# Where a Fourier layer's sixteen pixel transposes stand: twelve ahead of the forward stage, four inside it

## The reference, cut to what matters

```python
x = coords @ fc0_w + fc0_b                       # (32, 64, 64, 3) -> 32 channels
for sw, cw, cb in the four layers:
    x_ft = rfft2(x);  out = einsum('bixy,ioxy->boxy', x_ft[:, :, :20, :20], sw)
    x = gelu(irfft2(out) + einsum('bchw,oc->bohw', x, cw) + cb)      # exact gelu
x = gelu(x @ fc1_w + fc1_b) @ fc2_w + fc2_b      # one value per pixel
h = concat(cls_tok, x);  h += attention(layernorm(h));  h += experts(layernorm(h))
```

## Time and profile before

| | |
|---|---|
| median of 3 runs | 1129.65 us (1129.07 to 1131.33) |
| the profiled execution's own time | 1131.64 us |
| its span, first to last instruction | 1129.8 us, so 1.84 us lie around it |
| PE, DVE, ACT, POOL busy | 1024.6, 614.7, 410.1, 137.2 us |
| mean granted TensorE clock | 0.978 |

### The profile page before, as it was taken

The page is one execution under the profiler, slowest core; times in us unless marked ns, Lnnn a source line. Parts: engine busy times, 40 slices in busy tenths (PEclk is TensorE's granted clock), DMA queues, the critical chain, the costliest instruction groups (busy, mean ns, idle before and its releaser), DMA issues.

```text
span 1129.8 us, 36328 instructions
## 1 busy us (share of the span) xinstructions
PE 1024.6 (91%) x16860; PEld 654.0 (58%) x16860; DVE 614.7 (54%) x773; ACT 410.1 (36%) x554; POOL 137.2 (12%) x127
## 2 busy tenths in 40 slices
PE   4899899899989999999899899889999899689996
PEld 3676567567657633676576667567325788632221
DVE  2258455825844221458248455923144577769887
ACT  2332233223223486232232233223585778421100
POOL 6000000000000000000000000020000665334421
PEclk9999999999999999999999999999999899879998
DMA  5220130022021300310220130020011000000000
GB/s 187 89 75 3 62 94 12 3 89 75 3 74 53 115 6 22 118 32 3 89 75 3 44 103 21 3 90 16 2 25 43 1 1 2 2 1 1 1 10 10
DMA packets 25660, 46.75 MB, mean 41 GB/s; under 512 B 9437, under 2 KB 10488, under 8 KB 24869
## 3 DMA queue, kind: packets, MB, share of 16 engines
q1 hardware_dynamic: 24694, 43.49, 12.6%
q10 hardware_dynamic: 384, 0.66, 0.2%
q0 software_dynamic: 432, 0.29, 0.1%
HBM read 30.25 MB, written 10.89 MB: 36 GB/s over the span
## 4 chain that ended last, share of the span: by engine, by line
PE 69%; DVE 14%; issue 6%; ACT 4%; DMA 3%; POOL 2%; SPq 1%; ACTq 0%; POOLq 0%; DVEq 0%
PE PSALL L1288 22%; PE PSALL L1256 7%; DVE WORK L1494 6%; PE PSALL L1366 4%; PE PSALL L1279 4%; PE PSALL L1232 4%; PE PSALL L517 4%; PE PSALL L1151 3%; PE PSALL L1376 3%; PE PSALL L1165 3%; PE PSALL L420 3%; DMA WORK<-MIXED 2%; PE PSALL L505 2%; DVE WORK L1513 2%; PE PSALL L399 2%
## 5 line engine op out<-in xcount | busy, mean ns | idle before, releaser
L1513 DVE STREAM_TRANSPOSE WORK<-PSALL 128x1024 f32<-128x1024 f32 x128 | 152.4, 1230 | 292.9 <-PE PSALL L1256 292.9
L1288 PEld LDWEIGHTS PSALL<-EW,WORK 64*128 64x128 f32 x4096 | 250.0, 193 | 65.5 <-issue 48.3
L1288 PE MATMUL PSALL<-EW,WORK 64*128 64x128 f32 x4096 | 266.1, 283 | 12.8 <-DVE WORK L1513 12.8
L1416 ACT ACTIVATE X<-PSALL,TABLES 128x1024 f32<-128x1024 f32 x128 | 141.7, 1114 | 331.6 <-PE PSALL L1288 331.6
L1494 DVE STREAM_TRANSPOSE WORK<-PSALL 128x1024 f32<-128x1024 f32 x84 | 102.3, 1223 | 26.8 <-PE PSALL L1151 26.8
L1397 ACT COPY SPEC<-PSALL 128x400 f32<-128x400 f32 x64 | 53.9, 851 | 152.7 <-PE PSALL L1165 149.8
L1165 PEld LDWEIGHTS PSALL<-TABLES,WORK 128*64 128x64 f32 x2000 | 67.0, 138 | 65.7 <-DVE WORK L1494 53.2
L1165 PE MATMUL PSALL<-TABLES,WORK 128*64 128x64 f32 x2000 | 80.7, 228 | 23.1 <-DVE WORK L1494 19.9
L1485 DVE STREAM_TRANSPOSE WORK<-X 128x1024 f32<-128x1024 f32 x78 | 92.8, 1207 | 16.4 <-PE PSALL L1288 16.4
L1151 PE MATMUL PSALL<-WORK,DW 32*64 32x256 f32 x2496 | 95.8, 391 | 0.0
L697 POOL MEMSET SW<- 64x4160 f32 x1 | 3.6, 3559 | 725.0 <-PE PSALL L1240 725.0
(11 more groups left out here) (156 smaller groups left out, 1059.1 us busy)
## 6 DMA issues: line engine op xcount, KB each, us to landing
SW<-in_spec_w SPq DMA_DIRECT2D x160, 80.0 KB, 2.7
spec_scr<-MIXED SPq DMA_DIRECT2D x24, 400.0 KB, 3.3
SPEC<-spec_scr SPq DMA_DIRECT2D x32, 200.0 KB
WORK<-spec_scr SPq DMA_DIRECT2D x16, 200.0 KB
WORK<-MIXED SPq DMA_DIRECT2D x64, 40.0 KB
WORK<-in_coords_w SPq DMA_DIRECT2D x2, 1024.0 KB, 4.8
XC<-in_coords_c SPq DMA_DIRECT2D x2, 1024.0 KB, 7.2
hid_scr<-WORK SPq DMA_DIRECT2D x64, 8.0 KB
```

Of the source, the lines that this page charges most:

```text
L1288: m = pe.matmul(PS[2 * p + z][:, 2 * b * GRID:(2 * b + 2) * GRID], G[64 * z:64 * z + 64, n % 2, b, h:h + 4, :, c].rearrange("p q o -> p (q ...
L1416: nc.scalar.activation(X[:, n].rearrange("p b (z d) c w -> p d z b (c w)", z=2)[:, p, :, :, 2 * t * GRID:2 * (t + 1) * GRID], PSALL[:, 2 * ...
L1513: nc.vector.transpose(G[:, n % 2, 2 * x + y].rearrange("p h o v -> p o h v"), PSALL[:, 4 + 2 * x:6 + 2 * x, :].rearrange("p k (h o v) -> p ...
```

## The change

Twelve pixel transposes stand in the inverse stage: images 2 and 3 in slots 3 and 4, images 0 and 1 in slot 5, 4 and 5 in slot 6, and 6 to 11 in the last slot. The other four follow the row transposes of images 1, 4, 7 and 10. Each image of the first fourteen has a home of its own: a new tile `XPS` of 3 x 1024 columns is added for images 2 to 4 (and again 14, 15), images 0 and 1 lie in `work[:, 8192:10240]`, 5 to 7 in `MIXED`, 8 to 13 in `work[:, 0:6144]`. The waits follow the homes. As the order of the transposes is no longer that of the images, PE's waits go by `pixels_done`. The scratch for dynamic DMA is set to 4096 instead of being left at its default.

```diff
-EARLY, XP_RING = 3, 6
-PIXELS_IN_INVERSE = [[], [], [], [], [0, 1], [2], [], [3, 4, 5, 6]]
-PIXELS_AFTER = [[], [7], [8], [9], [10], [11], [12], [13], [14], [15], [], [], [], [], [], []]
+SPARE = 3
+PIXELS_IN_INVERSE = [[], [], [], [2], [3], [0, 1], [4, 5], [6, 7, 8, 9, 10, 11]]
+PIXELS_AFTER = [[], [12], [], [], [13], [], [], [14], [], [], [15], [], [], [], [], []]
+PIXEL_ORDER = [k for slot in PIXELS_IN_INVERSE + PIXELS_AFTER for k in slot]
...
+def pixels_done(k):
+
+    return max(PIXEL_ORDER.index(i) for i in range(k + 1)) + 1
...
-        pixel_homes = ([MIXED[:, 1024 * i:1024 * i + 1024] for i in range(EARLY)]
-                       + [work[:, 1024 * i:1024 * i + 1024] for i in range(XP_RING)])
-        XP = [(pixel_homes[k] if k < EARLY else pixel_homes[EARLY + (k - EARLY) % XP_RING])
-              .rearrange("p (h u c v) -> p h u c v", h=2, c=CH, v=2) for k in range(GIMG)]
+        XPS = sb("XPS", [128, SPARE * 1024])
+
+        pixel_homes = ([work[:, 8192:9216], work[:, 9216:10240]] + [XPS[:, 1024 * i:1024 * i + 1024] for i in range(SPARE)]
+                       + [MIXED[:, 1024 * i:1024 * i + 1024] for i in range(3)]
+                       + [work[:, 1024 * i:1024 * i + 1024] for i in range(6)] + [XPS[:, 0:1024], XPS[:, 1024:2048]])
+        XP = [home.rearrange("p (h u c v) -> p h u c v", h=2, c=CH, v=2) for home in pixel_homes]
...
             def two_columns():
-                cols.wait(xp_ready, 2)
+                cols.wait(xp_ready, pixels_done(1))
...
                 if s < GIMG:
-                    cols.wait(xp_ready, s + 1)
+                    cols.wait(xp_ready, pixels_done(s))
...
             def pixels_onto_partitions(k):
                 n, b = k // B4, k % B4
-                if k < EARLY + 4:
+                if k < 12:
                     turn.wait(x_ready, 4 * (n + 1))
                     if k == 0:
+                        turn.wait(ih_full, 6)
+                    if k == 5:
                         turn.wait(straight_in, 1)
                         for g in range(1, NG):
                             turn.wait(stored[g], 1)
-                    if k == EARLY:
+                    if k == 8:
                         turn.wait(x_full, 12)
                 else:
                     turn.wait(x_ready, 4 * (n + 1) - 4 * NG)
-                    if k == EARLY + 4:
+                    if k == 12:
                         turn.wait(x_full, 0)
-                    if k >= EARLY + XP_RING:
-                        cols.wait(c_full, columns_done(k - XP_RING))
+                    if k >= 14:
+                        cols.wait(c_full, columns_done(k - 12))
...
-    nc = bacc.Bacc("TRN2", target_bir_lowering=False, num_devices=1)
+    nc = bacc.Bacc("TRN2", target_bir_lowering=False, num_devices=1, dynamic_dma_scratch_size=4096)
```

## The result

The changed kernel took 1117.71 us (median of 4 runs, 1111.71 to 1119.4) beside 1130.33 for the kernel before: ratio 0.9879, 95% interval 0.9839 to 0.992. That is 12.6 us less; the median lies at the slow end of the range, 0.01 us above its 1117.7. Five more runs of the same kernel, on one chip with 16 runs of the kernel before, gave 1114.95 (1113.06 to 1115.84) against 1132.27: 17.3 us less, ratio 0.9844, interval 0.9828 to 0.9859, which is 16.0 to 19.5 us. A seventeenth run of the kernel before took 1188.31 us, at a mean clock of 0.838, and is left out of these numbers. The forecast was 17.2.

A forecast was written before the change was run, and what follows sets the result against it. DVE was taken to bound eight steps of each forward stage, PE the rest. 3.37 - 0.51 = 2.86 us per stage, six stages, 17.2 us: median 1112.5 us, range 1109.0 to 1117.7.

The forecast's parts named there:

- Step 1: Forward stage: five pixel transposes leave it, removing DVE's excess over PE's 1.80 us pace; gain 3.37 us per stage.
- the late ones: Forward stage: pixel transposes of images 13, 14, 15, behind row transposes 4, 7, 10; 0.17 us each, 0.51 per stage.
- Step 2: Forward stage: four pixel transposes stay; image 12's hidden in idle time, the other three cost 0.51 us per stage.
- the single row before: Earlier trace, forward stage: one pixel transpose following an idle DVE made the row transform at 199.82 start 0.17 us late.
- the upper bound, 0.46: Forward stage: most that each of three remaining pixel transposes could cost, 2.26 - 1.80 us, as in the dense stretch.
- Steps 3 and 5: Inverse stage: twelve pixel transposes fit DVE's idle time, and moved waits hold up no inverse transposes; cost nothing.
- Step 4: Inverse stage's last slot: six pixel transposes delay row transposes 0 and 1 without PE waiting; uncovered, up to 2.3 us per stage.
- the margin of 2.6 us: Last slot: time left between row transpose 1's end and PE's third column transform near 195.0; 2.6 us.
- the slower rival: Last slot: six transposes end too late and PE waits; at 2.3 us each 8.8 us lost, 1138.5; chance 0.03.
- Step 6: DMA scratch cut to a quarter: POOL's 13 loads might wait, 0 to 38 us on POOL; nothing on the path.
- Pace or busy time: Forward stage: gain reckoned by PE's 1.80 us start-to-start pace, 17.2 us, or by its busy time, 13.6 us (1116.1).
- the dear rival: Forward stage: three remaining pixel transposes cost 0.46 us each, gain only 11.9 us, 1117.7; chance 0.12.

## Why the prediction was right

The forecast was 17.2 us less, 1112.5 for the median; 12.6 less was measured at first and 17.3 with more runs. That the second number comes within 0.1 of the forecast is luck, as its interval is 16.0 to 19.5; the firmer ground is the 2.84 us per stage, which every trace of the changed kernel repeats within 0.02.

*Step 1, five transposes leave.* 3.37 us per stage. What was measured is that less the price of the late ones: with none of them, 26.70 - 23.38 = 3.32.

*Step 2, four stay.* Image 12 is hidden. The other three cost 0.16 each, where the single row before gave 0.17, and the upper bound, 0.46, showed when they stood close together. The lower one, 0 for a spaced one, showed nowhere; only in the idle time ahead of row transpose 2 does a transpose cost nothing. The sum of 2.86 per stage measured 2.84.

*Steps 3 and 5, the inverse stage and the moved waits.* In its eight slots no inverse transpose starts late: a clean layer lasts 95.09 us instead of 97.94 (537.18 to 635.12 before, 528.07 to 623.16 after), 2.85 less, all of it from the forward stage.

*Step 4, six in the last slot.* They end at 190.1 and the margin of 2.6 us was tested from both sides. This decides the slower rival: the place was well chosen, the price too, and the kernel stands a little over two transposes away from the edge.

*Step 6, the scratch.* No difference in POOL's issues or in the time. The prediction feared that a smaller ring might hold the loads back, from what the Trainium skill says of it (SBUF — State Buffer, SBUF size: 16 KiB per partition of DMA-descriptor ring, with no word on a smaller one). 13 loads of up to 66 KB, issued 0.53 us apart, were not held back.

*Pace or busy time.* By PE's busy time the gain would have been 13.6 us, by its pace 17.2. The rule quoted in the prediction says only that busy time misjudges; that the pace is the right measure comes from the 1.80 us of the earlier trace rows and is borne out here. PE is now busy for 23.59 us in the stretch, 0.34 less than the 23.93 of the earlier trace rows for the same instructions: the overlap that busy time leaves out. The first median of 1117.71 would have fitted the dear rival (1117.7); the trace shows that it is not that.

What the text underrated is the spread. It took 1 to 2 us from three runs within 2.3 us of each other. The real spread of either kernel is about 8 us (1111.71 to 1119.40 over nine runs, 1127.92 to 1136.19 over sixteen), so 0.4 us for the scatter of a median was too little, and the first median lies right at the upper end of the range, which reached that far only for the dear rival's sake.

## What to carry to other kernels

Where two engines take turns, compare their start-to-start times step by step, not their shares of the span: an engine busy for 54% overall was the bound for eight steps in each of six stages. Extra work for such an engine cost its full difference here when it came in a row (0.46 us), and about a third of that when each piece found the engine idle before it (0.16), so what cannot be moved out is best spread out, or put into an idle stretch that is already there. Before judging a gain of one or two per cent by its median, set each time beside its mean clock, and compare the stretch that was changed in the two traces.

## What was not expected of the hardware

TensorE's granted clock fell to the 1.2 GHz level for about 3.4 us at a time inside stretches that were otherwise at 2.4 GHz, not in every run but often at the same few places: in the first trace of the changed kernel at 20, 44, 388 and 448 us, in its second at 20, 44 and 388, in the kernel before at 392 and 736. Each such stretch in the network cost 1.1 to 1.6 us. In that first trace the one at 44 begins with the first matmuls behind two idle times of PE, 1.59 and 1.36 us; the kernel before has the same two (1.58 and 1.36) and no low stretch there. The copies of the modes within the chip's memory took between 2.45 and 3.39 us for the same bytes. Copies that landed later show as up to 0.6 us per layer, and their own length is only part of that: in two layers of the second pass the copy was the shorter one in the trace after (2.67 against 2.92 us, 2.46 against 2.94) and began later.
